# Audio tower on one core: the residual H and the routing weights pass through memory into rows of 64 tokens

## The reference

```
h = qrnn(conv(x))                       # gates z, f, o; a scan over t
h = h + gelu(long_conv(layernorm(h)))   # per channel, along t
h = h + moe(layernorm(h))               # 16 experts, top 2 of each token
# moe: picks and softmax weights of each token;
#      y_mean[e] = w2[e] @ mean over the tokens of expert e of silu(w1[e] @ x)
#      out[token] = sum over its 2 picks k of routing_w[k] * y_mean[pick k]
```

## Time and profile before

| | |
|---|---|
| median of 3 runs | 516.35 us |
| the profiled execution | 518.48 us, its span 516.7 us |
| mean granted TensorE clock | 0.862 of full |
| TensorE busy | 398.5 us (77%) |
| VectorE busy | 312.4 us (60%) |
| ScalarE busy | 218.4 us (42%) |
| GpSimd busy | 200.3 us (39%) |
| HBM | 34.86 MB read, 8.42 MB written |

### The profile page before, as it was taken

How to read it: one execution, slowest core, us unless ns; L and a number is a source line. 1 busy time by engine, 2 the same in 40 slices (tenths; PEclk the granted TensorE clock), 3 DMA queues, 4 the chain that set the end, 5 groups by cost and what they waited for, 6 DMA issues and landing times.

```text
span 516.7 us, 7312 instructions
## 1 busy us (share of the span) xinstructions
PE 398.5 (77%) x1929; PEld 269.6 (52%) x1930; DVE 312.4 (60%) x831; ACT 218.4 (42%) x423; POOL 200.3 (39%) x227
## 2 busy tenths in 40 slices
PE   8999999994998988313566530779988697799983
PEld 7888888883998965201352210334433243344562
DVE  3698888889488999520352310567744454367894
ACT  3335455552333665411533210457644453367420
POOL 2011111114101998777055775600066666510510
PEclk9999999998998995755566955799997988799998
DMA  6207443212209430822252121100191111100029
GB/s 183 58 1 187 120 118 109 77 56 72 79 1 283 111 92 5 258 86 56 99 138 77 51 58 41 41 5 2 34 338 46 46 41 41 41 15 1 1 72 242
DMA packets 53020, 43.68 MB, mean 85 GB/s; under 512 B 20686, under 2 KB 45980, under 8 KB 52732
## 3 DMA queue, kind: packets, MB, share of 16 engines
q1 hardware_dynamic: 44276, 32.09, 21.6%
q0 software_dynamic: 4416, 9.05, 6.4%
q10 hardware_dynamic: 4296, 2.15, 1.6%
HBM read 34.86 MB, written 8.42 MB: 84 GB/s over the span
## 4 chain that ended last, share of the span: by engine, by line
issue 33%; PE 28%; another core or an unknown queue 11%; DVE 11%; ACT 8%; POOL 5%; DVEq 3%; POOLq 0%; ACTq 0%
PE P L919 14%; PE P L852 5%; ACT P L1249 4%; DVE BIG L1679 3%; DVE H L1795 2%; PE P L889 2%; POOL rs L556 2%; PE P L1046 1%; DVEq L1673 1%; POOL XN L587 1%; ACT XN L1170 1%; DVE arena L1471 1%; POOL arena L584 1%; PE P L681 1%
## 5 line engine op out<-in xcount | busy, mean ns | idle before, releaser
L1679 DVE TENSOR_TENSOR BIG<-BIG,P 128x512 f32 x138 | 94.9, 688 | 105.0 <-issue 61.0
L919 PE MATMUL P<-w1T,arena 128*128 x276 | 143.5, 653 | 17.2 <-DVE BIG L1679 11.8
L919 PEld LDWEIGHTS P<-w1T,arena 128*128 128x128 f32 x276 | 52.0, 208 | 72.6 <-issue 72.2
L1249 ACT ACTIVATE P<-P 128x512 f32<-128x512 f32 x138 | 72.8, 580 | 1.6 <-PE P L919 1.5
L604 POOL DMA_INDIRECT XN<-table,arena x60 | 57.9, 965 | 40.0 <-issue 18.7
L1238 ACT COPY arena<-P 128x384 f32<-128x384 f32 (+1 forms) x48 | 22.4, 466 | 111.7 <-remote 49.7
L604 POOL DMA_INDIRECT arena<-table,arena x42 | 39.6, 943 | 64.5 <-PE P L919 47.2
L556 POOL TENSOR_TENSOR rs<-ve,mhalf 123x4 f32<-123x4 f32 x16 | 17.9, 1117 | 106.2 <-DVE ve L1340 106.2
L1087 ACT ACTIVATE arena<-P 128x492 f32<-128x492 f32 x48 | 27.8, 582 | 50.5 <-PE P L646 50.5
L604 POOL DMA_INDIRECT BIG<-table,arena x36 | 34.0, 944 | 20.5 <-issue 10.5
L646 PE MATMUL P<-xh,wh 128*128 128x498 f32 x144 | 41.9, 399 | 0.0
(11 more groups left out here) (241 smaller groups left out, 636.8 us busy)
## 6 DMA issues: line engine op xcount, KB each, us to landing
arena<-kpad SPq DMA_DIRECT2D x16, 492.0 KB, 4.1
XN<-in_L_ffn_w SPq DMA_DIRECT2D x1, 4096.0 KB
arena<-in_x SPq DMA_DIRECT2D x16, 224.0 KB
table<-XN SPq DMA_DIRECT2D x4, 896.0 KB
BIG<-table SPq DMA_DIRECT2D x1, 2048.0 KB
out<-H SPq DMA_DIRECT2D x8, 224.0 KB
out<-H ACTq DMA_DIRECT2D x8, 224.0 KB
BIG<-table SPq DMA_DIRECT2D x1, 1024.0 KB
```

The costliest lines, as they stand in the source:

```text
L919: mm = nc.tensor.matmul(bank[:, :], stat, w1T[:, bass.ds(e * FF, FF)], start=True, stop=True)
L1249: nc.scalar.activation(bank[:, :], bank[:, :], ACT.Silu).then_inc(silu_done, 1)
L1679: v.tensor_tensor(at, at, bank[:, :], ALU.add).then_inc(esum_step, 1)
```

## The change

`H` stays as it is through routing. Once the last `clear` is issued, SP writes all of `H` to the output's own memory, in the place of each token (8 transfers, runs of 512 B). It waits for them and reads the same memory back into `H` in another split: partition p gets the 64 tokens that lie in a row at 64p (2 transfers, 32 KB a partition). For R, SP waits for `R_ready`, writes `L` to the same memory as 16 floats a token in output order (1 transfer of 123 partitions, runs of 64 B), waits, and reads it back into `Ltmp` as 64 tokens of 16 floats a partition (1 transfer of 123 partitions, runs of 4 KB). All of this stands ahead of the load of `w2` on SP's queue.

TensorE's transposes of R read `Ltmp`, wait for `R_in` in place of `R_ready`, and come after tiles 50 and 55. VectorE waits for `H_in` before the first mix step. The mix itself has the same instructions. A store of 4 tokens is now one run of 2 KB a partition.

```diff
-        RT_AT = (23, 26)
+        RT_AT = (50, 55)
...
-        ov = out.rearrange("b t d -> t b d")
+        ov = out.rearrange("b t d -> (b t d)").rearrange("(p r d) -> p r d", p=T, r=B)
...
             clear(15, 6, 8)
+            by_t = out.rearrange("b t d -> t b d")
+            for g in range(NQ):
+                for lo, hi in ((0, SPLIT), (SPLIT, T)):
+                    sp.dma_start(by_t[lo:hi, g * QB:(g + 1) * QB], H[lo:hi, g * QB:(g + 1) * QB]).then_inc(H_out, 16)
+            sp.wait_ge(H_out, 2 * NQ * 16)
+            for lo, hi in ((0, SPLIT), (SPLIT, T)):
+                sp.dma_start(H[lo:hi], ov[lo:hi]).then_inc(H_in, 16)
+            sp.wait_ge(H_in, 32)
+            sp.wait_ge(R_ready, 1)
+            sp.dma_start(bass.AP(out.tensor, 0, [[E, T], [T * E, B], [1, E]]), L[0:T]).then_inc(R_out, 16)
+            sp.wait_ge(R_out, 16)
+            sp.dma_start(Ltmp[0:T], bass.AP(out.tensor, 0, [[B * E, T], [E, B], [1, E]])).then_inc(R_in, 16)
             sp.wait_ge(group_mm, EARLY_GROUPS)
...
                 if n in RT_AT:
-                    pe.wait_ge(R_ready, 1)
+                    pe.wait_ge(R_in, 16)
...
                         mm = nc.tensor.transpose(PRT[:, k * T:(k + 1) * T],
-                                                 L[0:T, b:b + HB].rearrange("p b e -> p (b e)"), ident[0:T, 0:T])
+                                                 Ltmp[0:T, b:b + HB].rearrange("p b e -> p (b e)"), ident[0:T, 0:T])
...
+            dve.wait_ge(H_in, 32)
             for n in range(2 * NHB):
                 dve.wait_ge(mix_mm, n + 1)
```

More of the change, by code:

```diff
@@ L399, in build @@
         R_ready = sem("R_ready")
+        R_out = sem("R_out")
+        R_in = sem("R_in")
+        H_out = sem("H_out")
+        H_in = sem("H_in")
         RT_mm = sem("RT_mm")
```

## The result

| | before | changed kernel |
|---|---|---|
| median | 516.15 us (515.16 to 519.0, 4 runs) | 527.99 us (527.27 to 529.38, 4 runs) |
| the profiled execution | 518.48 us, span 516.7 | 527.74 us, span 526.0 |
| mean granted TensorE clock | 0.862 | 0.852 |
| HBM | 34.86 MB read, 8.42 MB written | 39.39 MB read, 12.96 MB written |

The ratio is 1.0222, with a 95% interval of 1.0196 to 1.0248: slower by 11.8 us, where 531 us had been forecast, in a range of 512 to 562.

What follows compares the result with a forecast made beforehand. TensorE was taken to bound the tile stage without slack, DMA throughput only the end. 14.3 + 1.2 + 2.3 - 3.4 = +14.4 us on a span of 516.7 gave 531.1, say 531 us by the median; range 512 to 562.

Steps and rivals of the forecast that it cites:

- R is hidden: Rival, chance 0.12: R is back before TensorE needs it at tile 50, so no wait: 511.3 us.
- Place of the wait: TensorE reaches the wait for R behind tile 50 at about 367.5 us and stands still for 14.3 us.
- parts 5 and 6: Tiles 50 and 55: 14.3 us wait, 1.2 transposes, 2.3 clock; tiles 23 and 26: 1.7 us wait removed, worth nothing.
- R's way out, R's way back: R to memory on 3 engines, 34.9 plus 1.3 us, landed at 373.4; back 7.1 plus 1.3, at 381.8.
- a small run costs a whole one: Rival, chance 0.13: in R's way out a 64 B run costs 31 ns, wait 60.8 us, 577 us in all.
- the doubling: In R's way out, a read-modify-write below 512 B might double 13.3 ns a run to 26.6: 566 us.
- the line's price: DMA price of a run: 10.8 ns plus 0.0394 ns per byte, giving 13.3 ns for R's 64 B runs.
- The share beside R: Sign: while R goes out, the DMA share is near 3/16 = 0.19; near 1 would mean the prediction is wrong.
- The low clock: Behind the wait at tile 50, three tiles at clock 0.50 take 5.04 us against 2.74: +2.3 us.
- The end: Stores of 2 KB leave 3.7 us behind the last add in place of 7.0: gain 3.4 us, bounds 0 and 4.1.
- H's trip: H out from about 270.3 to 291 us, back by about 305, 32 us of cover before R: costs nothing.
- The wait with what hangs on it: At tile 50: 14.3 us of TensorE standing still, 1.2 of transposes behind it and 2.3 of lower clock.

Runs made afterwards that it cites:

- 4 KB back: Changed kernel with R's transfers cut at 112 rows and H read back as 16 transfers in runs of 4 KB: 518.42 us, ratio 0.9983 to the kernel before.
- R first: As 4 KB back, with R's way out and back put ahead of H's on SP's queue: 517.45 us, ratio 0.9981 to the kernel before.
- the change again: The changed kernel itself, unedited, run on another chip: 532.58 us, ratio 1.0247 to the kernel before.
- the place alone: The kernel before with only the transposes of R moved to tiles 50 and 55: 426.21 us beside 425.94, ratio 1.0001.

## Why the prediction was right

**The mechanism** is the predicted one: 3 engines for 123 rows, R late, all tiles from 51 on behind the wait. A cut at 112 takes the loss away and a cut at 122 enlarges it, which no rival without the split of the rows would do, and the shares of the ways back (0.19 and 0.12) count the engines. The rival *R is hidden* is false for this cut and true for the cut at 112, where 511.3 had been its time and 3.4 us of gain were measured in place of 5.1.

**Place of the wait.** TensorE came to tile 50's wait at 364.55 (378.48 - 13.93), 3 us sooner than the 367.5 predicted, as the wait and the transposes of tiles 23 and 26 no longer lie ahead of it. The prediction named both (parts 5 and 6) but put the 1.2 us of transposes behind the wait as a cost without taking them off in front of it: the wait should have been 14.3 + 1.7 + 1.2 = 17.2 us by its own working. This was an error of the sum; with the return at 381.8 the total is the same.

**R's way out, R's way back.** 32.1 us instead of 36.2, since a run of 64 B costs 11.7 ns and not 13.3; 8.8 us instead of 8.4. So TensorE resumed at 378.5, not 381.8. The extrapolated price was 14% too high. The rival *a small run costs a whole one*, 31 ns, is out by the same number. So is the doubling: the Trainium skill (DMA: Bandwidth & Descriptors, Specifications) has a read-modify-write below 512 B; the 26.6 ns that a doubling of the line's price would make aren't reached: 11.7 for 64 B and 12.2 for 32 B are below the line's own 13.3 or at its 12.1. No doubling of the line's price is seen; what such a run would cost without a read-modify-write no run shows.

**The share beside R** was named as 3/16 = 0.19 and is 0.35 on the way out, 0.19 only on the way back. By the packets' own times each of three engines is 1.85 times busy on the way out, so records of one engine overlap there. For runs this short the bytes a second, not the share, tell how fast an engine gets through: 16 GB/s with three engines, 11 with two.

**The low clock** behind the wait cost 2.2 us (4.91 - 2.74), predicted 2.3. The granted clock over those three tiles was 0.55 here, and 0.55 in the row that the prediction took the price from, not 0.50.

**The end.** 2.0 us gained instead of 3.4. The mis-sized term is the 2 KB write: 77.2% of 16 x 16 us / 1968 = 100.4 ns, where 91.5 was taken from reads of w2. 123 x 100.4 ns = 12.3 us is more than the 11.1 of the adds, so a queue of 1.2 us builds up again, and with it 3.7 becomes 4.9; seen were 5.0. In the two runs without trips the gain of the medians was 3.2 and 2.3, the place of the transposes included.

**H's trip** cost nothing, as predicted, but not by its sum: out it took 21.7 us, near the 20.7 predicted, back about 22 instead of 13.7, to about 312. 25 us of cover were left of the 32. On the chip where `L` comes at 272, there was none. `L` itself came later there in the three kernels with H's trip (272.0, 272.3 and 274.6 us) than in the one without (269.6); on the slower chips it didn't (339.0 and 338.7).

**The last 3.6 us** of the balance are not explained. The stretch of the last 54 gathers took 83.1 us before and 79.4 after. In the other traces of this length it is 80.7 (R cut at 112), 82.9 and 82.9 (no R trip, no trips), 83.5 (cut at 122), 80.2, 82.7 and 81.8 (4 KB back, R first, the change again). So it varies by as much without regard to the edit, and in all four traces of the faster chip it is 66.2. In this one profile it makes the balance smaller than what the terms of the change add up to: 14.9 - 2.0 = 12.9, where 14.4 was predicted, 9.3 is the balance, and 11.8 and 14.0 came by the medians.

**Where it was luck.** Two terms were mis-sized in opposite directions. The wait with what hangs on it was 17.8 in the sum and 14.9 in the trace, mostly the price of the small run; the gain of the stores was 3.4 and 2.0. The errors are 2.9 and 1.4 us, and half of the first is covered by the second. The forecast of 531 us is near 527.99 partly for this reason.

## What to carry to other kernels

Before a transfer is put on a path that something waits for, factor its row count: 123 rows in one piece had 3 of 16 engines, and two pieces of 112 and 11 rows took 9.3 us in place of 32.1. A trip through memory in a better layout can cost nothing at all, if its return is earlier than its user also on the fastest chip that the kernel will run on, not only in the profile at hand. For runs of 32 and 64 B count runs, not bytes (12 ns each on an engine); for writes from 2 KB on, count bytes; in between, a run of 512 B cost 31 ns and one of 2 KB 100.

## What the runs showed of the hardware

**One kernel, two times.** The kernel before has its median at 516 to 519 us beside the changed kernel and on two of the experiments' chips, and at 425.9 on the third. Windows of the kernel with the place alone, on that third chip (columns as in the earlier trace rows):

```profile
200.00:250.00 50.00, 38.29 (x262) 24.03 (x263) 31.55 (x113) 31.08 (x65) 38.30 (x37) 0.64 0.54 169
250.00:300.00 50.00, 48.14 (x152) 23.15 (x151) 36.74 (x52) 31.51 (x66) 38.11 (x40) 1.00 0.20 53
300.00:350.00 50.00, 50.00 (x161) 24.56 (x159) 36.14 (x54) 34.12 (x71) 37.81 (x41) 1.00 0.43 137
```

And the same windows of the kernel before, in its profile of 516.7 us:

```profile
200.00:250.00 50.00, 17.50 (x106) 10.19 (x107) 16.16 (x50) 14.12 (x30) 33.72 (x33) 0.57 0.35 105
250.00:300.00 50.00, 28.90 (x155) 17.08 (x154) 17.87 (x61) 19.42 (x38) 26.27 (x28) 0.67 0.33 98
300.00:350.00 50.00, 26.97 (x72) 12.16 (x73) 19.27 (x27) 16.19 (x34) 22.86 (x25) 0.74 0.13 34
```

Up to 200 us the two traces agree. In the next 150 TensorE is busy for 136.4 us in the one and 73.4 in the other: the standstills of ScalarE of up to 18.5 us have no counterpart on the fast chip, where its longest idle time from 200 to 345 us is 3.6. The trace names no semaphore of the kernel's own that ended them ("issue", "remote"), and their cause stays open. The difference goes on in the tile stage: the last 54 gathers take 66.2 us on the fast chip and 83.1 in the profile of 516.7 us.

**Long runs hold up gathers.** H's way back in runs of 32 KB, in the DMA view of the kernel with 4 KB stores, 263 to 287 us (packets, MB, share; then count, and us to landing). Behind it, the gathers beside H's way out in runs of 512 B, 241 to 262 us of the same kernel, and those with neither beside them, 263 to 287 us of the kernel with the place alone:

```profile
q1 hardware_dynamic: 150, 4.03, 73.2%
XN<-table,arena POOLq DMA_INDIRECT x15, 12.2
...
XN<-table,arena POOLq DMA_INDIRECT x18, 4.5
...
XN<-table,arena POOLq DMA_INDIRECT x15, 2.5
```

73.2% of 16 x 24 us / 123 runs are 2.3 us a run, 1.75 times the line's 1.3, and gathers issued meanwhile land after 12.2 us, against 4.5 us beside the runs of 512 B and 2.5 us with no burst. In runs of 4 KB, 248 ns, it is 1.44 times the line. R's way back, in 120 runs of 4 KB over three engines, took 13.4% of 16 x 9 us / 120 = 161 ns a run, and w2 91.5 ns for 2 KB over 16. So neither the length of a run nor the 16 engines alone explain H's price; why it is so high is open.
